# A transformer block on one core: MLP chunk loops written out, last chunk in four parts, two loads moved into attention, one GpSimd sum step exchanged

## What is computed

```
mod = silu(condition) @ Wada + bada
sh_a, sc_a, gt_a, sh_m, sc_m, gt_m = split(mod, 6)
xm = layernorm(x, g1, be1) * (1 + sc_a) + sh_a
x = x + gt_a * (causal_attention(xm, Wqkv) @ Wproj + bproj)
xm = layernorm(x, g2, be2) * (1 + sc_m) + sh_m
h = gelu(xm @ W1 + b1)
x = x + gt_m * (h @ W2 + b2)
```

## Time and profile before

| | us |
|---|---|
| median of 3 runs (2230.69 to 2244.35) | 2232.89 |
| profiled execution | 2236.31 |
| its span | 2234.1 |
| TensorE matmul busy (96% of the span) | 2154.2 |
| VectorE busy (58%) | 1286.7 |
| GpSimd busy (43%) | 965.7 |
| ScalarE busy (42%) | 929.2 |

### The profile page before, as it was taken

How to read it: one execution, slowest core, us unless ns; L and a number is a source line. 1 busy time by engine, 2 the same in 40 slices (tenths; PEclk the granted TensorE clock), 3 DMA queues, 4 the chain that set the end, 5 groups by cost and what they waited for, 6 DMA issues and landing times. The chain is left out here.

```text
span 2234.1 us, 31272 instructions
## 1 busy us (share of the span) xinstructions
PE 2154.2 (96%) x11326; PEld 1443.9 (65%) x11326; DVE 1286.7 (58%) x2872; ACT 929.2 (42%) x1780; POOL 965.7 (43%) x380
## 2 busy tenths in 40 slices
PE   6999999999999999999999999899999999999998
PEld 5888885454444545454444544677888888888886
DVE  4778876777777777777777754784313213133132
ACT  2111115566566656655655665335322222222221
POOL 2001007979799797988979773760000000000000
PEclk9999999999999999999999999999999999999999
DMA  6548346235261522625243222784101011011010
GB/s 235 206 151 266 127 168 158 63 76 120 54 138 46 119 66 63 149 49 131 52 112 80 59 77 63 247 319 155 67 37 57 0 56 56 0 56 56 0 38 19
DMA packets 129240, 222.96 MB, mean 100 GB/s; under 512 B 8526, under 2 KB 26006, under 8 KB 128920
## 3 DMA queue, kind: packets, MB, share of 16 engines
q1 hardware_dynamic: 107992, 179.38, 29.5%
q10 hardware_dynamic: 21120, 41.95, 5.1%
HBM read 146.31 MB, written 74.98 MB: 99 GB/s over the span
## 5 line engine op out<-in xcount | busy, mean ns | idle before, releaser
L1170 ACT ACTIVATE prob<-st 128x512 f32<-128x512 f32 (+3 forms) x1280 | 608.0, 542 | 387.2 <-PE st L1344 371.6
L1140 POOL TENSOR_TENSOR psum_k<-psum_k,prob 128x2048 f32<-128x2048 f32 (+1 forms) x150 | 670.8, 4472 | 21.0 <-ACT prob L1170 5.4
L1226 DVE TENSOR_REDUCE part<-mx 128x1 f32<-128x512 f32 x702 | 459.0, 685 | 107.0 <-PE mx L1324 104.0
L1344 PE MATMUL st<-q_st,k_st 98*128 98x512 f32 (+3 forms) x1280 | 489.8, 395 | 8.1 <-ACT prob L1170 4.1
L1324 PE MATMUL mx<-k_st,qx_st 96*128 96x512 f32 (+3 forms) x1189 | 465.7, 407 | 17.7 <-DVE part L1222 5.6
L1738 DVE TENSOR_TENSOR m_g_lo<-m_g,m_g_hi 128x512 fp32r<-128x512 f32 x128 | 88.6, 693 | 494.8 <-ACT m_g_hi L1652 494.8
L1344 PEld LDWEIGHTS st<-q_st,k_st 98*128 98x128 f32 x1280 | 242.7, 190 | 194.3 <-issue 103.1
L1324 PEld LDWEIGHTS mx<-k_st,qx_st 96*128 96x128 f32 x1189 | 224.0, 190 | 169.7 <-DVE part L1226 107.3
L1222 DVE CUSTOM_DVE_ANT_0 unused<-mx,mask_row 128x256 bf16<-128x256 f32 x487 | 230.6, 485 | 124.8 <-PE mx L1324 119.7
L1361 PE MATMUL o_ps<-prob,v_sb 128*32 128x512 f32 (+3 forms) x2560 | 285.6, 551 | 3.0 <-POOL prob L1123 3.0
L1648 ACT ACTIVATE m_g<-m_hid,vcol 128x512 f32<-128x512 f32 x128 | 88.2, 689 | 480.3 <-PE m_hid L1835 480.3
(11 more groups left out here) (168 smaller groups left out, 2593.5 us busy)
## 6 DMA issues: line engine op xcount, KB each, us to landing
k_st<-qk_scratch SPq DMA_DIRECT2D x96, 256.0 KB, 8.3
qx_st<-qk_scratch SPq DMA_DIRECT2D x96, 256.0 KB, 5.0
q_st<-qk_scratch SPq DMA_DIRECT2D x96, 256.0 KB
qk_scratch<-st_hi ACTq DMA_DIRECT2D x16, 1024.0 KB, 4.2
qk_scratch<-st_lo ACTq DMA_DIRECT2D x16, 1024.0 KB, 6.9
xs<-in_x_dram SPq DMA_DIRECT2D x8, 1024.0 KB, 8.7
v_sb<-v_scratch SPq DMA_DIRECT2D x8, 1024.0 KB, 15.4
o_scratch<-o_sb SPq DMA_DIRECT2D x32, 256.0 KB, 2.3
```

The costliest lines, as they stand in the source:

```text
L1140: nc.gpsimd.tensor_tensor(dst, src, prob[:, s % BUF, :, m:], ALU.add).then_inc(pool_added, 1)
L1170: nc.scalar.activation(prob[:, s % BUF, h, m:], st[n % RING][:, m:], ACT.Exp, scale=SCALE).then_inc(exp_done, 1)
L1226: nc.vector.tensor_reduce(most, bank[:, 0:w], AX.X, ALU.max).then_inc(mx_free, 1)
L1344: nc.tensor.matmul(st[n % RING][:, m:], k_st[u][0:MROWS, h, kt * P:(kt + 1) * P], q_st[0:MROWS, pos % 2, h, m:], start=True, stop=True).th ...
```

## The change

1. **MLP loops.** On SP, ScalarE, VectorE and TensorE the hardware loops are written out. TensorE no longer waits for its sums at a chunk's end; ScalarE waits for sum_ready before it overwrites the first four g tiles of the next chunk. The bias additions of finish move between VectorE's tiles 8 to 11 of the chunk (add_bias), and the product with the gate has two buffers.
2. **Last chunk.** The last three output tiles are computed block by block, and each block is stored by itself.
3. **Loads.** x of chunk 0 (E.x0) and the attention output of chunk 1 are loaded in the last head group, into space that the group has given free. GpSimd's low(2) no longer waits for the first norm.
4. **Table.** In POOLED[3], 11 and 12 become 12 and 13.

```diff
-    POOLED = {3: (0, 1, 2, 3, 4, 5, 6, 8, 9, 10, 11, 12), 2: (0, 1, 2, 3, 4, 5, 6, 8, 9), 1: (0, 1, 2, 4, 5), 0: ()}
+    POOLED = {3: (0, 1, 2, 3, 4, 5, 6, 8, 9, 10, 12, 13), 2: (0, 1, 2, 3, 4, 5, 6, 8, 9), 1: (0, 1, 2, 4, 5), 0: ()}
...
+                else:
+                    sp.wait_ge(p_ready, BATCH)
+                    sp.dma_start(E.x0[:, :, :], x[0:CH, :].rearrange("(t p) d -> p t d", p=P)).then_inc(K.x0_loaded, 16)
+                    steps_done(g, 2)
+                    sp.dma_start(E.o_in[1][:, :, :], K.o[0:KT, :, CH:2 * CH].rearrange("g p n -> p g n")).then_inc(K.o1_loaded, 16)
                 store_o(g, 2)
...
-            load_o(1)
-            load_x(0)
             load_x(1)
             load_o(2)
...
-            with nc.sync.Fori(0, NCH - 1) as n:
-                body(n, True)
-            body(NCH - 1, False)
+            for n in range(NCH - 1):
...
+            n = NCH - 1
+            for s in range(TT):
+                sp.wait_ge(out_ready, TT * n + s + 1)
+                sp.dma_start(out[n * CH + s * P:n * CH + (s + 1) * P, :], ms[:, s, :]).then_inc(out_stored, 16)
+            sp.wait_ge(out_stored, 16 * (n + TT))
...
-                if n >= 2:
-                    pool.wait_ge(xn_ready, TT * max(n - OB + 1, 1))
+                if n >= OB:
+                    pool.wait_ge(xn_ready, TT * (n - OB + 1))
...
-                act.wait_ge(used, HT * n + j + 1)
+                if j >= 4:
+                    act.wait_ge(used, (HT - 1) * n + j - 3)
+                elif n:
+                    act.wait_ge(sum_ready, TT * n)
...
-            dve.wait_ge(x_loaded[0], 16)
+            dve.wait_ge(K.x0_loaded, 16)
...
+            for n in range(1, NCH):
                 for j in range(HT):
                     tile(n, j)
-                xm_low(n + 1, xr)
-                b = n // (NCH // BATCH)
-                finish(n, K.gate[:, 1, bass.ds(b, 1), :], gbias[:, bass.ds(b, 1), :])
...
+                    if j >= HT - 2 * TT and j < HT - TT:
+                        add_bias(n, j - HT + 2 * TT)
+                if n < NCH - 1:
+                    xm_low(n + 1, xr)
+                finish(n)
...
-                if j < HT - 1:
-                    ins.then_inc(used, 1)
-                else:
-                    pe.wait_ge(sum_ready, TT * (n + 1))
-                    pe.sem_inc(used, 1)
+                for s in range(TT):
+                    multiply_tokens(n, j, s)
...
-            with nc.tensor.Fori(1, NCH) as n:
+            for n in range(1, NCH - 1):
                 for j in range(HT + LAG):
...
+            n = NCH - 1
+            for j in range(HT):
+                hidden(n, j)
+                if LAG <= j < HT - 2:
+                    multiply(n, j - LAG)
+            multiply(n, HT - 4)
+            for s in range(TT):
+                for j in range(HT - 3, HT):
+                    multiply_tokens(n, j, s)
```

More of the change, by code:

```diff
@@ L1689, in _ @@
             xm_high(1, xr)
-            with nc.scalar.Fori(1, NCH - 1) as n:
+            for n in range(1, NCH):
                 for j in range(HT):
                     tile(n, j)
-                act.wait_ge(xm_loaded, 16 * (n + 1))
-                xm_high(n + 1, xr)
-            for j in range(HT):
-                tile(NCH - 1, j)
+                if n < NCH - 1:
+                    act.wait_ge(xm_loaded, 16 * (n + 1))
+                    xm_high(n + 1, xr)
         @block.vector
@@ L1837, in hidden, with multiply_tokens @@
                 ins.then_inc(hid_ready, 1)
+            def multiply_tokens(n, j, s):
+                if s == 0:
+                    if j % KT == 0:
+                        pe.wait_ge(w_split, 4 * (j // KT) + 4)
+                    pe.wait_ge(g_ready, HT * n + j + 1 + 2)
+                if j == 0:
+                    pe.wait_ge(sum_free, TT * n + s + 1)
+                cols = slice(s * P, (s + 1) * P)
+                for k, (a, b) in enumerate(terms(g_hi[:, j % 4, cols], g_lo[:, j % 4, cols],
+                                                 w2_hi[j // KT][:, j % KT, :], w2_lo[j // KT][:, j % KT, :])):
+                    ins = nc.tensor.matmul(acc[s][:, :], a, b, start=(j == 0 and k == 0), stop=(j == HT - 1 and k == 2))
+                if j == HT - 1:
+                    ins.then_inc(sum_ready, 1)
+                elif s == TT - 1:
+                    ins.then_inc(used, 1)
             def multiply(n, j):
-                if j % KT == 0:
-                    pe.wait_ge(w_split, 4 * (j // KT) + 4)
-                pe.wait_ge(g_ready, HT * n + j + 1 + 2)
                 for s in range(TT):
-                    if j == 0:
-                        pe.wait_ge(sum_free, TT * n + s + 1)
-                    cols = slice(s * P, (s + 1) * P)
-                    for k, (a, b) in enumerate(terms(g_hi[:, j % 4, cols], g_lo[:, j % 4, cols],
-                                                     w2_hi[j // KT][:, j % KT, :], w2_lo[j // KT][:, j % KT, :])):
-                        ins = nc.tensor.matmul(acc[s][:, :], a, b, start=(j == 0 and k == 0), stop=(j == HT - 1 and k == 2))
-                    if j == HT - 1:
-                        ins.then_inc(sum_ready, 1)
-                if j < HT - 1:
-                    ins.then_inc(used, 1)
-                else:
-                    pe.wait_ge(sum_ready, TT * (n + 1))
-                    pe.sem_inc(used, 1)
+                    multiply_tokens(n, j, s)
             for n in range(2):
```

104 lines of the change are left out of this document (52 added, 52 removed).

## The result

| | us |
|---|---|
| changed kernel, median of 8 runs (2221.25 to 2226.18) | 2223.43 |
| before, median of 8 runs (2229.42 to 2244.35) | 2235.48 |
| ratio, with its 95% interval | 0.9946 [0.9929, 0.9963] |
| changed kernel again, beside the experiments, 6 runs (2212.24 to 2223.54) | 2219.35 |
| its ratio to 11 runs of before beside it (median 2238.17) | 0.991 [0.9889, 0.9931] |

The change makes the kernel faster by 12.1 us in the first comparison and by 18.8 us in the second. The forecast was -18.8 us and 2214.1 us, with a range up to 2223; the first median is 0.4 us outside. The means are 2237.1 us (before, the 46 runs beside the second comparison and the experiments; 2236.9 with the 8 of the first) and 2221.2 us (changed, all 14 runs): -15.9 us.

What follows compares the result with a forecast made beforehand. TensorE was taken to set the time nearly everywhere, so only its waits or work behind its last instruction pay. -7.6 - 4.3 - 4.0 - 2.9 = -18.8 us gave 2214.1 us against the median 2232.9; range 2207 to 2223.

Steps and rivals of the forecast that it cites:

- MLP loops (forecast -7.6): Seven MLP chunk boundaries: without drain and branch, 5.6 us idle and 2.0 us slow restart go; -5.6 if restart stays.
- 0.28 us at most: MLP chunk boundary: the most that the trace gives the loop's taken branch, cited against written-out code being slower.
- Rival 3: MLP chunk boundaries: a new wait there takes back the 7.6 us, giving 2221.7 us; chance 0.04.
- rival 5: Written-out MLP chunks: instruction stops of 4.33 us per new chunk, +26 us, 2240.1 us, slower than before; chance 0.03.
- Last chunk (forecast -4.3): Program end: no queue of sums on VectorE and a 256 KB last store landing in 2.3 us; -3 to -4.7.
- Loads (forecast -4.0): Projection start: 2.02 us stop for the residual sum goes, 4.22 us stop for chunk 1's norm halves; bounds 0, -6.2.
- Rival 2: First norm: GpSimd and VectorE collide, up to 3.6 us; taking the loads' 4.0 us gives 2218.1 us; chance 0.05.
- Table (forecast -2.9): Attention head groups: mask waits -3.0, three ScalarE waits of 0.39 gone, seven wider sums +0.19 each; bounds +0.7, -8.1.
- Both fall away: Attention: TensorE's 0.91 us wait for masking and 0.39 us wait for ScalarE, held by GpSimd's sum, both go.
- only three groups have this wait: Attention: in the other four of seven head groups the clock drops there, masking is done, and nothing is gained.
- if the three groups get such a slow stretch too: Table's unfavourable bound: clock drops of 1.2 us each in the three waiting groups, no longer hidden, make it +0.7.
- rival 1: Only MLP loops and end pay, -11.9, 2221.0 us; projection chain and clock drops may take the rest; chance 0.24.

Runs made afterwards that it cites:

- experiment 1: Changed kernel with the old table and the two loads behind the barrier, GpSimd's release kept: 2222.73 us, ratio 0.9936 to the kernel before.
- experiment 2: Changed kernel, written out, with TensorE again waiting for its own sums at each MLP chunk's end: 2223.56 us, ratio 0.9945 to before.
- experiment 7: Changed kernel with the two loads again behind the barrier, GpSimd's release kept, run twice: 2223.53 us (ratio 0.9947) and 2219.54 us (0.9926).
- experiment 8: Changed kernel with GpSimd's low part waiting for the first norm again, loads left in the last head group: 2223.02 us, ratio 0.9932.

## Why the prediction was right or wrong

**MLP loops (forecast -7.6): right.** The profiles show -7.8, and experiments 1 and 2 agree. The size came from the boundary, and so it held; the cause that the text named, the drain with its idle time and slow restart, is only half of it. By experiment 2 the drain makes 3.8 us of it and the loop 4.0. The "0.28 us at most" for the branch is what the jump back adds (0.86 - 0.58 us); that the first boundary too, without a jump back, pays 0.28 us for the loop was not seen. The Trainium skill, Runtime: NRT & Kernel Launch, section Instruction fetch mechanics, warns of the taken branch; the looped boundaries agree with the direction, but half of the loop's share lies where no jump back is, and whether the rest is a fetch, no run here shows. Rival 3 (a new wait at the boundaries) and rival 5 (written-out code stops) are dead: 87.04 us per chunk is pure work.

**Last chunk (forecast -4.3): right.** -4.6 in the profiles, 4.1 for the four parts and 0.5 for the second buffer, which the forecast left out. The small store lands in 2.0 us, the forecast had 2.3.

**Loads (forecast -4.0): the mechanism right.** The 2.02 us stop went, the 4.22 us one fell to 1.6, more than the half that was estimated, and the projection is shorter by 4.0 us over all profiles. That is the forecast's size, and in the profiles "the shift carries": nothing behind the projection takes it back. The means of the executions give 1 to 2 us, with an uncertainty of 1.0 to 1.4, and leave the rest open. Rival 2 did not come in the changed kernel: in the first norm the small steps take 0.16 us. It came in experiments 1 and 7, where GpSimd was released and the loads were late. The Trainium skill, SBUF — State Buffer, section Who interferes with whom, was cited against the edit. The trace agrees with it in direction (the page has no size for these operations): four operations of 0.69 us, 2.8 us, take 6.56 us in experiment 8 and 5.07 in the changed kernel, where GpSimd's two-input operations run beside them. With the loads early the rule came out in favour of the edit: the overlap moved to where it costs less.

**Table (forecast -2.9): the step that failed.** "There TensorE waits ... Both fall away" was right, and better than forecast: a group at full clock is 1.3 us shorter (131.1 to 129.8). Wrong was "only three groups have this wait. In the other four the granted clock drops there ... There nothing is gained": the drops were taken from the one profile as fixed to their groups, and as something that stays free when the wait beside it goes. They are not fixed, and with the new table a drop costs 1.6 us instead of 0.8, because the wait that took it up is gone; some also come at a new place, near 85 us. In the profiled pair this made the six groups 6.0 us longer, from 791.7 to 797.7; over all profiles they are 1.2 us shorter. The bound named it ("if the three groups get such a slow stretch too", +0.7), but the sum took the favourable value. The runs give 0.9998 [0.9986, 1.0009]. The second half of rival 1, "the clock may fall into the head groups that now wait", is this; its first half, that the projection's chain takes its gain back, the profiles do not show. (The sum itself, -3.0 - 1.17 + 1.33, is -2.8, not -2.9.)

**The level.** With -7.6, -4.3 and -4.0 as forecast and -1 in place of -2.9 the sum is -16.9, with -1.5 for the loads -14.4; the means give -15.9 with an uncertainty of 1.2 and do not decide between them. The first comparison gave -12.1 and the second -18.8. That these two differ by 6.7 us for one pair of kernels is itself a part of the miss: the median of three runs that the forecast started from, 2232.9 us, lay 4 us below the mean of 46. The changed kernel's mean, 2221.2 us, is nearly rival 1's 2221.0, but that agreement is luck: rival 1 has -11.9 us from a level 4 us too low. The range was also narrower than its own terms: it was said to take in the bounds, while the smallest terms added up to 2225.0 us, above its end at 2223 and above the 2223.4 measured first.

## What to carry to other kernels

On an engine that sets the time, price an edit by the gaps it closes between that engine's instructions: hardware loop and self-wait at 1.1 us per boundary, and a last store cut into parts, came out within 0.5 us of the forecast. Here a wait inside dense code also hid drops of the clock, and its removal was worth less than its length; look at several executions before tying a drop to one group, and compare group lengths at full clock and clock means apart. Where single terms of 1 to 4 us are at stake and executions spread over 10 us, read them from stretches of the profile, and ask the time only for the sum.

## What was not expected of the hardware

- The granted clock fell between seven and thirteen times in attention, in stretches in which TensorE is busy 97% of the time, in the six full head groups always at one of three places of a group, but not in the same groups in two executions of the same kernel: two adjacent groups of one execution are 132.8 and 129.8 us long with the same work. This makes most of the spread of the runs (2212 to 2226 us for the changed kernel, at mean clocks of 0.991 to 0.984).
- At a chunk boundary TensorE's wait for its own last matmuls costs 0.31 us and makes the next 36 matmuls 0.25 us slower; the hardware loop adds about 0.5 us, of which 0.28 us are there already at the step into the loop (0.58 us idle against 0.30), without a jump back.
- Six MLP chunks written out, with 768 matmuls each, cost nothing: the larger instruction queue moves 90 packets and 1.47 MB in all, against 72 and 1.18 before, and TensorE does not stop once in 609 us.
- A drop of the clock where TensorE would otherwise have waited cost nothing here: two adjacent groups of before, one with a drop and one with the mask wait, both take 131.14 us.
